# One block for the recurrent passes, one for add, normalisation and first batch-normalised layer, and one wait taken out of the eigenvalue passes

## The reference, cut to what matters

```python
# layer 0: a spectral layer; it needs the eigenvectors of the normalised Laplacian
_, U = jnp.linalg.eigh(L_norm)
# layer 1: two graph convolutions, then four recurrent passes over windows of p nodes
for p in range(1, MAX_SKIP + 1):                      # MAX_SKIP = 4
    nw = Tv // p
    wins = h[:, :nw * p, :].reshape(Bv * nw, p, Hd)
    last = _lstm_last(Wih[p-1], Whh[p-1], bih[p-1], bhh[p-1], wins)
    h = h.at[:, jnp.arange(nw) * p + (p - 1), :].set(last.reshape(Bv, nw, Hd))
# layer 2: aggregate, linear, batch norm, relu, linear, batch norm
agg = jnp.einsum('nm,bmd->bnd', A_hat, features)
h = jax.nn.relu(_batchnorm(agg.reshape(-1, d) @ W1.T + b1, g1, be1))
out = _batchnorm(h @ W2.T + b2, g2, be2)
# layer 3: causal attention with an additive mask
```

## Time and profile before

| | |
|---|---|
| median of 3 runs | 5159.02 us |
| profiled execution | 5158.07 us |
| its span, first to last instruction | 5156.1 us |
| PE (TensorE) busy | 3458.6 us, 67%, granted clock 0.675 of full speed |
| DVE (VectorE) busy | 3826.3 us, 74% |
| ACT (ScalarE) busy | 1601.7 us, 31% |
| POOL (GpSimd) busy | 31.9 us |
| recurrent passes | 4118 to 4659 us of the span |
| add of the recurrent result | 4659 to 4684 us |
| layer normalisation | 4684 to 4717 us |
| first batch-normalised layer | 4717 to 4804 us |

### The profile page before, as it was taken

One profiled execution on the slowest core, in us unless ns is written; L12 is line 12 of the kernel. 1 busy time (PEld: TensorE's weight loads), 2 busy tenths in 40 slices (PEclk: granted clock), 3 DMA queues, 4 the chain that ended last, 5 costly groups with the idle time before them and its releaser, 6 DMA issues. The chain is left out here.

```text
span 5156.1 us, 58802 instructions
## 1 busy us (share of the span) xinstructions
PE 3458.6 (67%) x10754; PEld 2181.0 (42%) x10777; DVE 3826.3 (74%) x24187; ACT 1601.7 (31%) x5460; POOL 31.9 (1%) x50
## 2 busy tenths in 40 slices
PE   4777777777777678866666664420479977885667
PEld 3555555666655577742222222210334423322334
DVE  7988889998999999988999999999543122214444
ACT  2444443333333333323222220000023253324454
POOL 0000000000000000000000000000000000000000
PEclk6555555555555555567887786655589989997889
DMA  0000000000000000000000000000200000000000
GB/s 9 1 1 1 1 1 1 1 1 1 1 1 1 1 1 1 1 1 1 1 1 1 1 1 1 1 0 0 56 0 1 1 0 0 0 0 0 0 14 19
DMA packets 14132, 15.86 MB, mean 3 GB/s; under 512 B 571, under 2 KB 10214, under 8 KB 13798
## 3 DMA queue, kind: packets, MB, share of 16 engines
q1 hardware_dynamic: 13798, 12.48, 0.9%
HBM read 8.28 MB, written 4.19 MB: 2 GB/s over the span
## 5 line engine op out<-in xcount | busy, mean ns | idle before, releaser
L231 PE MATMUL ps<-dot_parts,ones 128*128 128x2 f32 x766 | 224.6, 363 | 355.1 <-DVE dot_parts L407 354.0
L211 PE MATMUL ps<-ident,vectors 128*128 128x128 f32 x1148 | 344.3, 438 | 125.7 <-DVE vectors L460 125.7
L231 PEld LDWEIGHTS ps<-dot_parts,ones 128*128 128x128 f32 x766 | 192.0, 311 | 542.1 <-DVE dot_parts L407 541.5
L1518 PE MATMUL ps<-h_features,WihT 128*128 x504 | 295.6, 747 | 49.9 <-ACT gates_skip L1549 27.2
L599 ACT ACTIVATE sturm_signs<-sturm_products,sign_bias 128x576 bf16<-128x576 f32 x160 | 123.9, 775 | 613.2 <-DVE products_mark L624 613.2
L277 ACT ACTIVATE refl<-ps,tiny 128x1 f32<-128x1 f32 x511 | 133.4, 261 | 520.7 <-PE ps L221 340.0
L356 DVE CUSTOM_DVE_ANT_0 products<-ps,UT 128x511 f32<-128x511 f32 (+58 forms) x589 | 257.8, 479 | 34.8 <-PE ps L211 31.1
L356 DVE CUSTOM_DVE_ANT_0 products<-ps,U 128x499 f32<-128x499 f32 (+62 forms) x559 | 240.0, 471 | 26.6 <-PE ps L211 23.1
L211 PEld LDWEIGHTS ps<-ident,vectors 128*128 128x128 f32 x1148 | 191.7, 213 | 158.6 <-DVE vectors L460 158.1
L291 ACT ACTIVATE vectors<-WihT,refl 128x4 f32<-128x4 f32 (+2 forms) x383 | 115.0, 300 | 430.3 <-DVE refl L413 376.7
L679 DVE TENSOR_TENSOR sturm_products<-x_times_p,e_times_p 128x64 f32<-128x64 f32 x1120 | 244.2, 218 | 0.0
(11 more groups left out here) (520 smaller groups left out, 9274.2 us busy)
## 6 DMA issues: line engine op xcount, KB each, us to landing
out_dram<-x SPq DMA_DIRECT2D x16, 256.0 KB, 2.3
adj<-in_adj_dram SPq DMA_DIRECT2D x1, 1024.0 KB, 5.2
l2w_in<-in_L_gnn_W_dram SPq DMA_DIRECT2D x2, 128.0 KB
Wqkv<-in_L_gnn_Wqkv_dram SPq DMA_DIRECT2D x1, 192.0 KB
L_gnn_W<-in_L_gnn_W_dram SPq DMA_DIRECT2D x2, 64.0 KB
L_gnn_Wg<-in_L_gnn_Wg_dram SPq DMA_DIRECT2D x2, 64.0 KB
x<-in_x_dram SPq DMA_DIRECT2D x4, 0.5 KB
L_gnn_Wo<-in_L_gnn_Wo_dram SPq DMA_DIRECT2D x1, 64.0 KB
```

Of the source, the lines that this page charges most:

```text
L211: ins=nc.tensor.transpose(XR[:,t*P:(t+1)*P],XG[:,t,X_:X_+1].broadcast_to([P,P]),ident[:])
L231: nc.tensor.matmul(dots(m),ones[:],dp[:],start=True,stop=True).then_inc(dot_ps,1)
L1518: ins=nc.tensor.matmul(shaped(bank(u,g)),WihT[:,(p-1)*4+g,:],nodes(j*2+u,s),start=True,stop=s==0)
```

## The change

It has four parts. (1) In the eigenvalue sweeps, the wait ahead of `older` is for `sc_at` alone, no longer for the last row of products too. (2) `lstm_pass`, called four times with a loop in each, becomes `recurrent_layer`: one block, all 72 steps written out in one list, with the semaphores counted through. The tail of a step now comes after the gates of the next step in the list, also across iterations and passes. The input product of a step waits for the gates of two steps before, and at a window's first step for those windows of the pass before that wrote its columns (`outs_needed`). (3) `add_transposed` for the recurrent result, `layernorm_relu` and the first block of `batchnorm_layers` become one block: TensorE transposes straight from HT, VectorE adds and takes statistics batch by batch, coefficients are made for groups of four batches, ScalarE normalises, and TensorE aggregates straight from H. A later group's transposes, additions and normalisation are written between the products of the group before. The GpSimd staging is gone, and the first half of the pre-activations is kept in HT's memory. (4) The loops of the second linear layer are written out.

The diff, without the removed bodies and without the vector operations that equal those of L1403 to L1418:

```diff
@@ -629,7 +629,7 @@
                         end=poly[:,(h-1)%2,BLK]
                         if not first:
 
-                            v.wait_ge(swp,max(p_at,sc_at))
+                            v.wait_ge(swp,sc_at)
                             r.inc(nc.vector.scalar_tensor_tensor(out=older[:],in0=poly[:,(h-1)%2,BLK-1],scalar=SIGN_BIAS,in1=sc[:],op0=ALU.add,op1=ALU.mult))
                             older_at=r.at()
...
@@ -1478,109 +1478,98 @@
-def lstm_pass(nc, sem, psum, p, HT, WihT, WhhT, gate_bias):
...
+def recurrent_layer(nc, sem, psum, HT, WihT, WhhT, gate_bias):
+    I,F_,G,O=range(4)
+    GATES=(I,G,F_,O)
     flat=HT[:].rearrange("p b n -> p (b n)")
+    whole=lambda p: N%p==0
+    width=lambda p: 512 if whole(p) else 2*(N//p)
+    batches=lambda p: p if whole(p) else 2
+    def nodes(p, ch, s):
+        seg=flat[:,ch*batches(p)*N:(ch+1)*batches(p)*N]
+        if whole(p): return seg[:,s::p]
+        return seg.rearrange("p (b n) -> p b n",n=N)[:,:,s:s+p*(N//p-1)+1:p]
+    def shaped(p, a):
+        return a if whole(p) else a.rearrange("p (b n) -> p b n",b=2)
+    steps=[(p,j,s,u) for p in range(1,MAX_SKIP+1) for j in range(B//batches(p)//2) for s in range(p) for u in range(2)]
+    out_before=[0]
+    for p,j,s,u in steps: out_before.append(out_before[-1]+(s==p-1))
+    passes_out=[0]
+    for p in range(1,MAX_SKIP+1): passes_out.append(passes_out[-1]+B//batches(p))
+    def outs_needed(p, ch):
+        if p==1: return 0
+        return passes_out[p-2]+-(-(ch+1)*batches(p)//batches(p-1))
+        sb1=lambda n,s: c.enter_context(nc.sbuf_tensor(n,s,F32))
+        gt=sb1("gates",[P,2,4,N]); C=sb1("cell2",[P,2,N]); th=sb1("tanh_c",[P,2,N]); h2=sb1("state2",[P,2,N]); fa=sb1("forget",[P,2,N]); ia=sb1("input",[P,2,N])
+        gates_ps=sem("gates_ps"); gates_sb=sem("gates_sb"); cell=sem("cell"); tc=sem("tanh_c"); st=sem("state"); outd=sem("window_out"); loc=sem("lstm_parts")
+        bank=lambda p,u,g: psum[4*u+g][:,0:width(p)]
             @block.tensor
+                for n,(p,j,s,u) in enumerate(steps):
+                    if u: continue
+                    for v_ in range(2):
+                        q=n+v_
+                        if q>=2: pe.wait_ge(gates_sb,q-1)
+                        if s==0 and outs_needed(p,2*j+v_): pe.wait_ge(outd,outs_needed(p,2*j+v_))
+                        for g in GATES:
+                            if s==0 and g==F_: continue
+                            ins=nc.tensor.matmul(shaped(p,bank(p,v_,g)),WihT[:,(p-1)*4+g,:],nodes(p,2*j+v_,s),start=True,stop=s==0)
+                            if s==0: ins.then_inc(gates_ps,2 if g==G else 1)
+                    if s==0: continue
+                    for v_ in range(2):
+                        q=n+v_
+                        pe.wait_ge(st,q-1)
+                        for g in GATES:
+                            nc.tensor.matmul(bank(p,v_,g),WhhT[:,(p-1)*4+g,:],h2[:,v_,0:width(p)],start=False,stop=True).then_inc(gates_ps,1)
             @block.scalar
+                def tail(n):
+                    p,j,s,u=steps[n]; w=width(p)
+                    act.wait_ge(cell,n+1)
+                    nc.scalar.activation(th[:,u,0:w],C[:,u,0:w],ACT.Tanh,scale=0.5).then_inc(tc,1)
+                    if s==p-1:
+                        act.wait_ge(st,n+1)
+                        nc.scalar.activation(nodes(p,2*j+u,s),shaped(p,h2[:,u,0:w]),ACT.Copy,scale=0.5).then_inc(outd,1)
+                for n,(p,j,s,u) in enumerate(steps):
+                    if n>=2: act.wait_ge(st,n-1)
+                    for i,g in enumerate(GATES):
+                        if s==0 and g==F_: continue
+                        act.wait_ge(gates_ps,4*n+i+1)
+                        k=(p-1)*4+g
+                        ins=nc.scalar.activation(gt[:,u,g,0:width(p)],bank(p,u,g),ACT.Tanh,bias=gate_bias[:,0 if g==G else 1,k:k+1],scale=1.0 if g==G else 0.5)
+                    ins.then_inc(gates_sb,1)
+                    if n: tail(n-1)
+                tail(len(steps)-1)
+                act.wait_ge(outd,out_before[-1])
             @block.vector
+                k=Steps(loc)
+                def tail(n):
+                    p,j,s,u=steps[n]; w=width(p)
+                    v.wait_ge(tc,n+1)
+                    if s==0 and n>=2: v.wait_ge(outd,out_before[n-1])
+                    nc.vector.scalar_tensor_tensor(out=h2[:,u,0:w],in0=gt[:,u,O,0:w],scalar=1.0,in1=th[:,u,0:w],op0=ALU.add,op1=ALU.mult).then_inc(st,1)
+                for n,(p,j,s,u) in enumerate(steps):
+                    w=width(p); g_=lambda g: gt[:,u,g,0:w]
+                    v.wait_ge(gates_sb,n+1)
+                    if n>=2: v.wait_ge(tc,n-1)
+                    if s==0:
+                        nc.vector.scalar_tensor_tensor(out=C[:,u,0:w],in0=g_(I),scalar=1.0,in1=g_(G),op0=ALU.add,op1=ALU.mult).then_inc(cell,1)
+                    else:
+                        k.inc(nc.vector.scalar_tensor_tensor(out=ia[:,u,0:w],in0=g_(I),scalar=1.0,in1=g_(G),op0=ALU.add,op1=ALU.mult))
+                        v.wait_ge(cell,n-1)
+                        k.inc(nc.vector.scalar_tensor_tensor(out=fa[:,u,0:w],in0=g_(F_),scalar=1.0,in1=C[:,u,0:w],op0=ALU.add,op1=ALU.mult))
+                        v.wait_ge(loc,k.at())
+                        nc.vector.scalar_tensor_tensor(out=C[:,u,0:w],in0=fa[:,u,0:w],scalar=0.5,in1=ia[:,u,0:w],op0=ALU.mult,op1=ALU.add).then_inc(cell,1)
+                    if n: tail(n-1)
+                tail(len(steps)-1)
+                v.wait_ge(st,len(steps))
...
@@ -1614,11 +1603,11 @@
-def batchnorm_layers(nc, sem, psum, ident, H, HQ, AhT, W1T, W2T, cols, X):
+def batchnorm_layers(nc, sem, psum, ident, HT, H, HQ, AhT, W1T, W2T, cols, X):
-        Pm=sb1("pre1",[P,2,B,N]); st1=sb1("bn_stats1",[P,2,B,6]); st2=sb1("bn_stats2",[P,B,6]); ag=sb1("bn_aggr",[P,3,2]); co=sb1("bn_coef",[P,8,3]); scl=sb1("bn_scale",[P,3]); bia=sb1("bn_bias",[P,3])
+        Pm=[HT,sb1("pre1",[P,B,N])]; st1=sb1("bn_stats1",[P,2,B,6]); st2=sb1("bn_stats2",[P,B,6]); ag=sb1("bn_aggr",[P,3,2]); co=sb1("bn_coef",[P,8,3]); scl=sb1("bn_scale",[P,3]); bia=sb1("bn_bias",[P,3])
@@ -1648,44 +1637,113 @@
-            hs=c2.enter_context(nc.sbuf_tensor("bn_h_in",[P,2,NT,D],F32)); a=c2.enter_context(nc.sbuf_tensor("bn_agg",[P,2,N],F32))
+            sb2=lambda n,s: c2.enter_context(nc.sbuf_tensor(n,s,F32))
+            a=sb2("bn_agg",[P,2,N]); bs=sb2("ln_bn_2",[P,2,NT,GROUP,6]); ls=sb2("ln_stats_2",[P,2,8,NT,GROUP])
+            MEAN,DIF,VAR_,Y_,Q,RS_,NB=range(7)
+            tps=sem("bn0_turned_ps"); added=sem("bn0_added"); stats=sem("bn0_ln_stats"); step=sem("bn0_ln_step"); var_ready=sem("bn0_ln_var"); root=sem("bn0_ln_root"); coef=sem("bn0_ln_coef"); h_ready=sem("bn0_h_ready")
+            aps=sem("bn1_agg_ps"); asb=sem("bn1_agg_sb"); pps=sem("bn1_ps"); psb=sem("bn1_sb"); sts=sem("bn1_stats")
+            TURN,AGG,PRE=psum[0:2],psum[2:4],psum[4:8]
+            def ahead(b):
+                g,i=divmod(b,GROUP)
+                return [g*GROUP+GROUP+2*i+k for k in range(2)] if i<2 and g+1<B//GROUP else []
-                @block.gpsimd
-                            nc.gpsimd.tensor_copy(hs[:,u],batch(H,j*2+u)).then_inc(stg,1)
                 @block.tensor
                 def _(pe):
+                    def turned(b):
+                        if b>=2: pe.wait_ge(added,b-1)
+                        for t in range(NT):
+                            ins=nc.tensor.transpose(TURN[b%2][:,t*P:(t+1)*P],HT[:,b,t*P:(t+1)*P],ident[:])
+                        ins.then_inc(tps,1)
+                    def first_linear(b):
+                        pe.wait_ge(asb,b+1)
+                        if b>=2: pe.wait_ge(psb,2*(b-1))
+                        for f in range(2):
+                            nc.tensor.matmul(PRE[2*(b%2)+f][:],W1T[:,f*P:(f+1)*P],a[:,b%2],start=True,stop=True).then_inc(pps,1)
+                    for b in range(GROUP): turned(b)
+                    for b in range(B):
+                        pe.wait_ge(h_ready,(b+1)*NT)
+                        if b>=2: pe.wait_ge(asb,b-1)
+                        for t in range(NT):
+                            ins=nc.tensor.matmul(AGG[b%2][:],H[:,t,b,:],AhT[:,t,:],start=t==0,stop=t==NT-1)
+                        ins.then_inc(aps,1)
+                        for q in ahead(b): turned(q)
+                        if b: first_linear(b-1)
+                    first_linear(B-1)
                 @block.scalar
                 def _(act):
+                    def roots(g):
+                        act.wait_ge(var_ready,g+1)
+                        nc.scalar.activation(ls[:,g%2,Y_],ls[:,g%2,VAR_],ACT.Sqrt).then_inc(root,1)
+                    def normalise(b):
+                        g,u=divmod(b,GROUP)
+                        act.wait_ge(coef,g+1)
+                        for t in range(NT):
+                            nc.scalar.activation(H[:,t,b,:],X[:,t,b,:],ACT.Relu,bias=ls[:,g%2,NB,t,u:u+1],scale=ls[:,g%2,RS_,t,u:u+1]).then_inc(h_ready,1)
+                    def kept(b):
```

(57 more changed lines are left out.)

136 lines of the change are left out of this document (19 added, 117 removed).

## The result

The changed kernel takes 5041.55 us, the median of 4 runs (5039.33 to 5050.13), against 5159.21 us for the kernel before in the same comparison: a ratio of 0.9775, 95% interval 0.9758 to 0.9792, 117.7 us less. The forecast was 5058 us and 101.4 us less, with a range of 5036 to 5082. The profiled execution takes 5039.33 us, its span is 5037.6 us where it was 5156.1: 118.5 us to account for.

What follows compares the result with a forecast made beforehand. The rebuilt stages were taken as bound by chains between engines and barriers, the sweeps by VectorE. 21.6+41.6+38.2 = 101.4 us off 5158.07 gives 5056.7, with 0.95 for the median 5058 us; range 5036 to 5082.

Steps and rivals of the forecast that it cites:

- The wait in the sweeps: Eigenvalue sweeps, VectorE: `older` needs L675, one instruction further back, saving 0.14 us 150 times; 21.6 us in all.
- The lower bound, 0.07 on top of the 0.14: Sweeps: if the wait instruction adds its 0.07 to the 0.14 of issue, 0.11 us is saved each, 17 us.
- The rival that the wait costs nothing: Sweeps: each instruction waits for the one before anyway, or `sc` is as late; 5080 us, chance 0.12.
- Recurrent passes: The four passes as one written-out block: 25.0+7.0+0.7+5.8+2.2+0.9 = 41.6 us saved.
- I keep the 5.40: Pass 2: the second state product still takes 5.40 us, some at the lower clock; an iteration takes 25.8 us.
- I take it unchanged, as the idle stretches ahead of them are unchanged: Recurrent passes: TensorE's clock behind idle stretches, in 18 second state products, was assumed to stay as before.
- The bound of 32 us either way: Recurrent passes: 18 second state products behind idle stretches, each losing or gaining 1.8 us (5.40 against 3.60).
- The second term: Pass 1, ScalarE as the chain: with one table load, a step takes (8.98-1.28)/2 = 3.85 us.
- The new block: Add to first batch-normalised layer: 145 us become 106.8, saving 38.2 us; bounds 33 and 41.
- The rival of a block in series: New block: engines keep written order, so three groups each show 10.3 us; 5089 us, chance 0.06.
- The written-out second layer: Second linear layer: its loop registers are off the chain, so 0 us saved, at most 1.
- Written-out code as a loss: TensorE in the new blocks: written-out code comes too slowly, at 0.06 us each 120 us lost; 5178 us, chance 0.02.

Runs made afterwards that it cites:

- the repeat: The changed kernel run again with no edit, beside other experiments on one chip: 5046.25 us, 0.9792 of the kernel before, 107.9 us less.
- e8_coef_late: The changed kernel with a group's coefficients and first normalisation one aggregation later on VectorE and ScalarE: 5057.71 us, 0.9815 of the kernel before.

## Why the prediction was right, and where it was off

It was right in sign, size and place: 101.4 us forecast, 117.7 and, in the repeat, 107.9 measured; 5041.55 us lies in the range, nearer its lower end.

- **The wait in the sweeps.** 20.0 us alone against 21.6, and 21.1 us in the eigenvalue block itself: `older` stands 0.32 us behind L675 rather than behind L679, and 0.18 to 0.19 behind L679. Whether that is the old 0.32 counted from L675, as the forecast had it, or 0.05 for the wait instruction on top of the 0.14 of neighbours, the runs can't tell: both give 0.19. The lower bound, 0.07 on top of the 0.14, falls. The rival that the wait costs nothing falls too: an instruction recorded at 0.22 us is followed after 0.14 if nothing waits for it, and each of two waits had a price of its own. The prediction had told the Trainium skill (page "VectorE: DVE Perf Modes", section "The DRAIN you can't avoid") as if its rule held for every instruction. That section also says that an instruction that isn't held starts earlier, and the 0.14 us here agree with that; what the rows don't bear out for these 128x64 tiles is that a semaphore costs nothing extra, as in that section's eight copies.
- **Recurrent passes.** 51.5 us against 41.6. The structure came as forecast: one table load, the 0.88 and most of the 1.54 idle us gone from pass 2, the 3.43 kept, no gap between passes. Two terms were off. The step "I keep the 5.40", with "I take it unchanged, as the idle stretches ahead of them are unchanged", failed in this execution: 3.70 in pass 2, four times 1.7 = 6.8 us. An iteration is 24.02 = 25.8-1.8. In pass 3 the clock took 4.9 us more than before, in pass 4 3.5 less, so against the forecast the 18 products gave 6.8-4.9+3.5 = 5.4 us of the 9.9 (against the kernel before 25.8-19.2 = 6.6, as its four of pass 2 took 5.30 to 6.71). The repeat shows it as a matter of the execution, not of the change: there the products' excess was 27.5 us, the forecast's assumption nearly kept, and the passes took 496.9 us, 43.5 less than before. The bound of 32 us either way was the right kind of doubt. The second term: ScalarE's waits for the state are 0.84 us, not 0.85 and 0.93, and the gates start 0.09 us before the copy's end, where the table load stood between them; a step of pass 1 takes 3.72 us, not 3.85, 14 times 0.13 = 1.8 us. The remaining 2.7 us, most of it in pass 3, weren't followed.
- **The new block.** 39.4 us against 38.2. Step by step: first aggregation after 13.5 us (13.3 forecast), then 92.4 us (93.5; a batch's four transposes take 0.44, not 0.56), 2.9 us of cover at a group change (3), no idle stretch of TensorE there. The rival of a block in series falls. `e8_coef_late` shows that the margin is real and small: one aggregation later, and 11.5 us were lost.
- **The written-out second layer.** 3.0 us in the stretch from it on, not 0 to 1. An iteration takes 5.31 us, 5.48 before, so the written-out code gave some 0.17 us each of eight times, 1.4 of the 3.0; another 1.0 lies in the attention (235.7 us before, 234.7 here), whose code is unchanged.
- **The unchanged code** gave 4.2 us in this execution, for which no forecast from one trace can stand.
- **Written-out code as a loss.** Falls in all kernels: in no new block is an idle stretch of TensorE put down to its sequencer, but at the start (1.10 us ahead of the passes, 8.58 ahead of the new block, barrier and clear included).

## What to carry to other kernels

When code is rearranged, price the waits that remain, not only those that go. Here the best of the change was next to it: the same tails, one place earlier, gave another 85 us, because a wait of TensorE costs its length and often some time at the lower clock behind it, 1.3 and 1.8 us on average in two executions here. On VectorE a semaphore wait on the neighbour cost 0.13 us a place and the second semaphore 0.05; over 155 and 150 places that is 20.0 and 7.7 us. And ask of every forecast term that rests on a granted clock whether it would come out the same if nothing were changed.

## What the runs showed of the hardware that was not expected

- The clock behind an idle stretch of the same length is not a constant of the kernel. Second products of eight records took 3.70, 5.40, 6.4 or 6.7 us behind 3.43 us of idle, in one kernel, in two executions.
- A product that reads every fourth column takes twice as long. Pass 4's first 28 records take 25.36 us, 0.91 each; pass 2's 16 take 7.61, 0.48 each, both of 512 columns, both at full clock. Every third column also costs: 16 records of 340 columns take 7.41 us, 0.46 each, against 0.31 for the state products, which read neighbours.

```profile
4305.53 7.41 PE L1522 MATMUL ps<-h_features,WihT 128*128 128x340 f32 x16
4312.77 2.46 PE L1529 MATMUL ps<-state,WhhT 128*128 128x340 f32 x8
```

  The Trainium skill (page "SBUF — State Buffer", section "Door 1: The DMA port swizzle") says that accesses run at full bandwidth if at least two fall into a line of 16 bytes; every fourth float32 is one to a line, every second one two. The rows agree. For every third column an estimate by that page is a factor of 1.5: of four such columns two share a line and two stand alone, (2+2x2)/4; measured 0.46/0.31. The page's next words, that one can stride for free by 4 float32, don't hold for these products.
- A table load takes 1.28 us and nothing more: the gates start at its end, and the load at 4093.7 ahead of gates at 4095.0. The Trainium skill (page "ScalarE: Activation LUTs", section "What ACT_TABLE_LOAD costs") adds a drain of about 1.38 us to each switch of sets. No such time shows here: not in the loop before, where the same set is loaded again, and not where the set changes. The load at 4093.7 follows work whose last table was the square root's, and so does the attention's first load, from 4811.34 to 4812.62 us in the changed kernel, right behind the instruction before it; its first exponential starts at 4812.63.
